# A recurrent block with an MLP and an FP4 gate: the MLP's down projection with the weight stationary, its sum turned by VectorE and through HBM

## The chip, the cores and the metric

The kernel runs on one core of a Trainium2 chip. The metric is the device time of one execution in microseconds (us). TensorE, VectorE, ScalarE, GpSimd and SyncE are called PE, DVE, ACT, POOL and SP, as in the profile; SP issues every DMA of this kernel.

## The reference

Input x has 4 sequences of 1024 tokens with 256 channels. In short:

```
xn = layernorm(x)
x1 = xn + linear_attention(rmsnorm(xn) ...) @ Wo      # 8 heads, chunks of 128 tokens, a carried state
h  = rmsnorm(x1) * mlp_norm_w
s  = x1 + (silu(h @ Wgate) * (h @ Wup)) @ Wdown       # 256 -> 1024 -> 256: the MLP
q  = fp4_linear(xn, w_gate), fp4_linear(xn, w_up)     # 256 -> 704, both operands rounded to FP4 in groups of 16
g  = silu(fp4_linear(silu(q0) * q1, w_down))          # 704 -> 256: the gate
out = x + s * g
```

The change touches the product with `Wdown` and the sum `x1 + ...` behind it.

## The kernel before

The work falls into blocks of 512 tokens (4 chunks of 128), 8 blocks in all. A first stage, up to about 600 us, does layer norm and attention for every block and leaves what the second stage needs in HBM: `kept` (x1 and its factor), `kept_xq` and `kept_h2` (rounded xn and normed x1, each turned in 32 x 32 pieces so that a load puts channels on partitions). The second stage, which the change is about, is one function `networks(n, final)` on each engine, called for n = 0 to 7. There is no scheduler: the order of work on each engine is the order of the program's text, engines meet at semaphores, and SP issues its DMAs strictly in the order in which its own text lists them, waiting in front of each for the semaphores named there.

All products are made of three fp32r matmuls of high and low halves (`split_product`, L250 to L259). In one block n of the second stage PE does, for each chunk c of 128 tokens:

- `gate_up4(n, c)`: the FP4 gate and up products of chunk c, 4 times 6 matmuls of 352 columns;
- `gate_up(n, 2c)` and `gate_up(n, 2c+1)`: slices f = 2c and 2c+1 (128 of the 1024 hidden channels) of the MLP's gate and up products, each over all 512 tokens with the weight stationary: 6 matmuls of 512 columns for gate, 6 for up;
- `down(n, f)` for f = 2c-1 and 2c (L801): the hidden slice f, times `Wdown`, added into PSUM banks `B_MLP` and `B_MLP + 1`. Here the activation `hmT` is stationary, one 128-token chunk at a time, and 256 columns of `wdown` move: 4 chunks times 3, so 12 matmuls of 256 columns for one f. The result lies with tokens on partitions;
- `down4(m)`: the FP4 down projection of the chunk m = 4n + c - 2, two chunks late (`LAG4 = 2`).

`down(n, 7)` ends the block's sum, then `gate_up4(n+1, 0)` begins the next one.

DVE in the same block rounds the hidden values of the FP4 branch (`quantize_scale`, `quantize_apply`, `quantize_constants`, `quantize_add`, `quantize_subtract`, `quantize_done`), multiplies gate and up of both branches (`mlp_product`, L1598 to L1601; `product4`, L1608 to L1612) and makes the low halves (`mlp_lo`, L1605; `hq_lo`, L1618; `xT_lo_of`, L1537). PE's `gate_up(n, f)` waits for `mlp_product(n, f-1)` before its up half, since there is one bank for up, and `down(n, f)` waits for `mlp_lo(n, f)`. At the end of a block DVE adds the MLP's sum to `x2b` (x1, loaded by SP) straight out of PSUM, in one instruction (L1696); POOL then multiplies by the gate and adds x.

The FP4 hidden values make a trip through HBM for each chunk m, `exchange4(m)` on SP (L507 to L520): the store of chunk m (L511), then a wait for that store and for `hq_lo(m-1)` by DVE, since the landing buffer is used again, then four loads (L519):

```
sp.wait_ge(h4_quantized, m + 1)
sp.dma_start(through.rearrange("a p x -> p a x"), h4_turned_sb).then_inc(hq_stored, 16)
sp.wait_ge(hq_stored, 16 * (m + 1))
...
    sp.wait_ge(hqT_ready, m)
```

`hq_lo(m-1)` for the last chunk of a block, m = 4n + 3, stands in DVE's text in the first chunk of the next block. Behind `exchange4(4n + 3)` SP issues the four loads of a later block's `kept_h2` (`load_turned`, L483 to L485).

Of the kernel before, what the change touches and what calls it, by code (L numbers as in the profile page):

```python
# [5 lines left out]
ALU = mybir.AluOpType  # L6
ACT = mybir.ActivationFunctionType
AX_X = mybir.AxisListType.X
F32 = mybir.dt.float32
# [4 lines left out]
P = 128  # L14
BANK = 512
QUAD = 32
QUADS = P // QUAD
# [41 lines left out]
def build(nc, x, attn_w, Wq, Wk, Wv, Wo, out_w, mlp_w, Wgate, Wup, Wdown, w_gate, w_up, w_down, out):  # L59
    batches, tokens, D = x.shape  # L60
    HD = Wq.shape[1]
    H = HD // P
    KD = D // P
    INTER = Wgate.shape[1]
    FT = INTER // P
    N4 = w_gate.shape[0]
    T4 = -(-N4 // P)
# [3 lines left out]
    CH = BANK // P  # L71
    TB = CH * P
    HALVES = tokens // TB
    BLOCKS = batches * HALVES
    STEPS = HALVES * H
# [12 lines left out]
    moved = nc.dram_tensor("moved", (QUADS, P, 2 * CH * QUAD), F32).ap()  # L88
    kept_xq, kept_h2 = (nc.dram_tensor(name, (BLOCKS, QUADS, P, KD * CH * QUAD), F32).ap()
                        for name in ("kept_xq", "kept_h2"))  # L90
    kept_h4 = nc.dram_tensor("kept_h4", (2, QUADS, P, T4 * QUAD), F32).ap()
    PIECE_OF = ((1, 0), (1, 1), (0, 0), (0, 1), (2, 0), (2, 1))
    PIECE4 = (N4, N4, N4, N4, T4 // 2 * D, T4 // 2 * D)
# [3 lines left out]
    with ctx:  # L97
# [3 lines left out]
        def sem(name):  # L101
            return ctx.enter_context(nc.semaphore(name))
# [14 lines left out]
        wdown = r_q[:, :].rearrange("p (a f n) -> p a f n", a=2, f=FT)  # L117


        r_h = sb("r_h", [P, 2 * 2 * KD * TB], F32R)  # L120
# [8 lines left out]
        hmT = hid_r.cut(2, 2, TB)  # L129
# [60 lines left out]
        def turned(tile, k):  # L190

            return tile.rearrange("p (a k c t) -> p k c a t", a=QUADS, k=KD, c=CH)[:, k]

        def landed(tile, k):

            return tile.rearrange("p (b k c t) -> p k c b t", b=QUADS, k=KD, c=CH)[:, k]
# [8 lines left out]
        def in_quads(tile):  # L205
            return tile.rearrange("p (a x) -> p a x", a=QUADS)
# [21 lines left out]
        xb = two.cut(CH, D)  # L228
        res = two.cut(CH, D)
        g4 = two.cut(CH, D)  # L230
        hq_in_last = xq_in[:, 0:QUADS * T4 * QUAD].rearrange("p (a x) -> p a x", a=QUADS)
        hqT_last = r_k[:, 0:2 * T4 * P].rearrange("p (a f n) -> p a f n", a=2, f=T4)
        two.at = x2_end
# [17 lines left out]
        def split_product(pe, out_ap, weight, activation, kinds, first, last, skip=False):  # L251

            for n, (wp, ap) in enumerate(PRODUCTS):
                a, b = activation(ap), weight(wp)
                if kinds == "weight stationary":
                    a, b = b, a
                done = pe.matmul(out_ap, a, b, start=first and n == 0, stop=last and n == 2,  # L259
                                 skip_group_check=skip)  # L260
            return done
# [77 lines left out]
        hq_stored, hq_loaded = sem("hq_stored"), sem("hq_loaded")  # L339
        out4_done, g4_ready = sem("out4_done"), sem("g4_ready")  # L340
        mlp_done, sum_read = sem("mlp_done"), sem("sum_read")
        product_ready, res_ready, out_stored = sem("product_ready"), sem("res_ready"), sem("out_stored")
        dve2 = sem("dve2_done")
        TURNS = 2 * KD
# [31 lines left out]
        with nc.Block() as block:  # L376
            @block.sync
            def _(sp):
# [125 lines left out]
                sp.wait_ge(xT_ready, TURNS)  # L504
                load_turned(h2_in, kept_h2[1], h2_loaded)

                def exchange4(m):  # L507

                    through = kept_h4[m % 2]
                    sp.wait_ge(h4_quantized, m + 1)  # L510
                    sp.dma_start(through.rearrange("a p x -> p a x"), h4_turned_sb).then_inc(hq_stored, 16)  # L511
                    sp.wait_ge(hq_stored, 16 * (m + 1))
                    if m == LAST4 - 1:
                        sp.wait_ge(xT_ready, (BLOCKS - 1) * TURNS + KD)
                    elif m:
                        sp.wait_ge(hqT_ready, m)
                    landing = hq_homes(m)[0]
                    for q in range(QUADS):
                        sp.dma_start(landing[q * QUAD:(q + 1) * QUAD],  # L519
                                     through[q].rearrange("(b p) x -> p b x", b=QUADS)).then_inc(hq_loaded, 16)  # L520

                for n in range(BLOCKS):
                    exchange4(n * CH)
                    if n == 0:
                        sp.wait_ge(wdown_ready, 2)
                        sp.dma_start(xb, x_blocks[0]).then_inc(xb_loaded, 16)
                    if n == 2:
                        sp.wait_ge(h2_turned, BLOCKS + 1)
                        sp.dma_start(kept_h2[BLOCKS - 1].rearrange("a p x -> p a x"),
                                     leaving.rearrange("p a i x -> p a (i x)")).then_inc(h2_stored, 16)  # L530
                    exchange4(n * CH + 1)
                    if n == 0:
                        sp.dma_start(x2b, kept[0][:, :, 0:D]).then_inc(xb_loaded, 16)
                    else:
                        sp.wait_ge(res_ready, n)
                        sp.dma_start(out_blocks[n - 1], res).then_inc(out_stored, 16)
                        sp.dma_start(xb, x_blocks[n]).then_inc(xb_loaded, 16)
                        if n == BLOCKS - 1:
                            sp.wait_ge(x2_stored, 16 * (BLOCKS + 1))
                        sp.dma_start(x2b, kept[n][:, :, 0:D]).then_inc(xb_loaded, 16)  # L540
                    exchange4(n * CH + 2)
                    if n + 2 < BLOCKS:
                        sp.wait_ge(xT_ready, (n + 1) * TURNS + KD)
                        load_turned(xq_in, kept_xq[n + 2], xq_loaded)
                    if n == 1:
                        sp.wait_ge(x2_ready, BLOCKS + 1)
                        sp.dma_start(kept[BLOCKS - 1], x2).then_inc(x2_stored, 16)
                    if n < BLOCKS - 1:
                        exchange4(n * CH + 3)
                    if n + 2 < BLOCKS:  # L550
                        sp.wait_ge(xT_ready, (n + 1) * TURNS + TURNS)
                        sp.wait_ge(h2_stored, 16 * (n + 4))
                        load_turned(h2_in, kept_h2[n + 2], h2_loaded)
# [40 lines left out]
            def _(pe):  # L594
# [205 lines left out]

                def down(n, f):  # L801
                    if f == 0:
                        pe.wait_ge(sum_read, n + 1)
                        pe.wait_ge(wdown_ready, 1)
                        pe.wait_ge(h4_ready, 1)
                    if n == 0 and f == FT // 2:
                        pe.wait_ge(wdown_ready, 2)
                    pe.wait_ge(hmT_ready, n * FT + f + 1)
                    for c in range(CH):
                        done = split_product(pe, ps[:, B_MLP + c // 2, (c % 2) * D:(c % 2 + 1) * D],  # L810
                                             lambda a: wdown[:, a, f, :],
                                             lambda a: hmT[:, f % 2, a, c * P:(c + 1) * P],
                                             "activation stationary", f == 0 and c % 2 == 0, f == FT - 1, skip=True)
                    if f == FT - 1:
                        done.then_inc(mlp_done, 1)
# [384 lines left out]
            def _(dve):  # L1200
# [128 lines left out]
                def turn_blocks(to, data, done_sem):  # L1329

                    for k in range(KD):
                        done = dve.transpose(turned(to, k), by_quads(data, k))
                    done.then_inc(done_sem, 1)
# [293 lines left out]
                                          hqT[:, HI, f0:f1, :].bitcast(F32), ALU.subtract).then_inc(hqT_ready, 1)  # L1627

                dve.sem_inc(sum_read, 1)
                dve.sem_inc(out_stored, 16)  # L1630
                product4(0, 0, 0)
                xT_lo_of(0, range(KD, TURNS))
# [4 lines left out]
                def wdown_lo(i):  # L1637
                    dve.wait_ge(wdown_hi, i + 1)
                    part = slice(i * FT // 2, (i + 1) * FT // 2)
                    dve.tensor_tensor(wdown[:, LO, part, :], raw_wdown[:, part, :], wdown[:, HI, part, :].bitcast(F32),  # L1640
                                      ALU.subtract).then_inc(wdown_ready, 1)

                DVE_BLOCK = CH * (SCALE_STEPS + ROUND_STEPS)

                def networks(n, final):
                    mine = Tally(n * DVE_BLOCK)
                    for c in range(CH):
# [32 lines left out]
                            x2_factor(BLOCKS + 1, before)  # L1680
                        if (n, c) == (2, 0):
                            dve.wait_ge(h2_ready, BLOCKS + 1)
                            dve.wait_ge(o_turned, STEPS - PLAIN - 1)
                            turn_blocks(leaving.rearrange("p a i x -> p (a i x)"), xq_new, h2_turned)
                        if c == 0:
                            product4(n, 1, 0)
                        quantize_subtract(data, mine)
# [3 lines left out]
                    if not final:  # L1691
                        xT_lo_of(n + 1, range(KD, TURNS))
                    dve.wait_ge(mlp_done, n + 1)
                    dve.wait_ge(xb_loaded, 32 * n + 32)
                    dve.wait_ge(out_stored, 16 * n + 16)
                    dve.tensor_tensor(res, ps[:, B_MLP:B_MLP + 2, :].rearrange("p a (c d) -> p (a c) d", d=D),  # L1696
                                      x2b, ALU.add).then_inc(sum_read, 1)
                    if not final:
                        product4(n + 1, 0, 0)
                        product4(n + 1, 0, 1)  # L1700
# [40 lines left out]
```

## Time and profile before

| | us |
|---|---|
| median of 3 runs (1065.27 to 1066.4) | 1065.48 |
| the profiled execution's own time | 1066.6 |
| its span, from the first to the last instruction | 1064.5 |
| PE busy in the span | 1053.9 (99%) |
| DVE busy | 908.8 (85%) |
| ACT busy | 528.1 (50%) |
| POOL busy | 47.4 (4%) |

A busy time is the time in which at least one instruction of the engine runs; a matmul's duration in the profile is that of a pipeline, so the spacing of matmuls is read from when groups of them begin in the timeline, and not from their mean duration. The share of the granted clock is 0.999 over the span. All times in the rows are of one profiled execution, in us from the span's start.

### The profile page before, as it was taken

Reading aid. Unit: us, or ns where it says so; the run is one execution under the profiler, and the core shown is the slowest. Engines: PE = TensorE matmul, PEld = TensorE weight load, DVE = VectorE, ACT = ScalarE, POOL = GpSimd, SP = SyncE. Lnnn points to the kernel's source line nnn. Section 1 sums busy time; section 2 is a strip of 40 time slices with the busy share of each in tenths; the row PEclk is TensorE's granted clock in tenths of the full one; section 3 lists DMA queues with packets and bytes.
Section 4 is the critical chain, followed back from the end, with each engine's and each line's share of the span. In section 5 each row is a group of like instructions: output and inputs, shape, how many; then the busy total and the mean of one; then the engine's idle time right before and its main releaser. Section 6 shows DMA issues by size and latency. Waiting matters only on the chain.

```text
span 1064.5 us, 18767 instructions
## 1 busy us (share of the span) xinstructions
PE 1053.9 (99%) x6794; PEld 961.5 (90%) x6794; DVE 908.8 (85%) x1887; ACT 528.1 (50%) x1490; POOL 47.4 (4%) x68
## 2 busy tenths in 40 slices
PE   9999999999999999999999999999999999999998
PEld 5999999989999989989999889999999999999997
DVE  6788888888888888888888798888888888889887
ACT  6664655756656546557555634443333333243332
POOL 0000000000000000000000000101001010101010
PEclk9999999999999999999999999999999999999999
DMA  7445355455464553653544623253433233423213
GB/s 237 149 159 174 108 173 168 138 157 166 134 192 133 165 171 115 187 170 123 171 148 162 194 66 99 80 158 93 121 90 119 85 120 97 122 84 92 87 57 112
DMA packets 166173, 143.08 MB, mean 134 GB/s; under 512 B 28737, under 2 KB 162881, under 8 KB 166081
## 3 DMA queue, kind: packets, MB, share of 16 engines
q1 hardware_dynamic: 166080, 141.88, 42.7%
q8 instruction: 54, 0.88, 0.4%
q14 instruction: 39, 0.31, 0.1%
HBM read 77.27 MB, written 64.57 MB: 133 GB/s over the span
## 4 chain that ended last, share of the span: by engine, by line
PE 88%; DMA 6%; DVE 2%; ACT 2%; SPq 2%; issue 1%; DVEq 0%
PE ps L259 69%; PE ps L713 5%; PE ps L757 4%; PE ps L751 4%; PE ps L737 4%; DMA moved<-work 3%; DMA r_gate<-moved 2%; SPq L409 1%; PE ps L839 1%; PE ps L598 1%; SPq L481 1%; DMA work<-kept_w 1%; DMA work<-in_L_attn_hidden_states 0%; ACT work L922 0%; DVE work L1473 0%
## 5 line engine op out<-in xcount | busy, mean ns | idle before, releaser
L259 PE MATMUL ps<-r_k,r_gate_up 128*128 128x512 f32 x768 | 185.2, 391 | 0.5 <-DVE r_k L1537 0.5
L259 PEld LDWEIGHTS ps<-r_k,r_gate_up 128*128 128x128 f32 x768 | 141.5, 188 | 27.9 <-issue 0.7
L259 PE MATMUL ps<-r_o,onT 128*128 128x256 f32 x768 | 107.0, 289 | 0.4 <-DVE onT L1265 0.4
L259 PE MATMUL ps<-r_h,r_k 128*128 128x512 f32 (+1 forms) x393 | 105.2, 403 | 0.0
L259 PEld LDWEIGHTS ps<-r_q,r_v 128*128 128x128 f32 x768 | 99.7, 191 | 5.0 <-DVE r_v L1605 0.3
L259 PE MATMUL ps<-r_q,r_v 128*128 128x256 f32 x768 | 102.3, 283 | 0.0
L259 PE MATMUL ps<-r_h,r_q 128*128 128x512 f32 x384 | 98.2, 391 | 0.0
L946 ACT ACTIVATE work<-ps 128x128 f32<-128x128 f32 x256 | 67.0, 276 | 62.8 <-PE ps L757 62.7
L259 PE MATMUL ps<-r_v,r_h 128*128 128x512 f32 x384 | 97.4, 390 | 0.0
L259 PEld LDWEIGHTS ps<-r_o,onT 128*128 128x128 f32 x768 | 95.8, 190 | 0.8 <-DVE onT L1265 0.7
L922 ACT ACTIVATE work<-ps 128x512 f32<-128x512 f32 x64 | 38.3, 599 | 109.3 <-PE ps L259 109.1
L1121 ACT ACTIVATE r_v<-work 128x512 fp32r<-128x512 f32 x64 | 40.5, 633 | 99.8 <-DVE work L1601 99.7
L259 PEld LDWEIGHTS ps<-r_h,r_q 128*128 128x128 f32 x384 | 72.1, 188 | 16.5
L259 PEld LDWEIGHTS ps<-r_v,r_h 128*128 128x128 f32 x384 | 72.1, 188 | 15.0
L1508 DVE TENSOR_TENSOR work<-ps,work 128x128 f32<-128x128 f32 x192 | 55.7, 290 | 26.6 <-ACT work L960 17.1
L259 PEld LDWEIGHTS ps<-r_h,r_k 128*128 128x128 f32 x393 | 68.2, 189 | 11.1
L1117 ACT ACTIVATE work<-ps 128x512 f32<-128x512 f32 x64 | 38.3, 598 | 79.1 <-PE ps L259 79.1
L259 PE MATMUL ps<-r_gate,r_k 128*128 128x352 f32 x384 | 71.8, 322 | 0.0
L259 PE MATMUL ps<-r_up,r_k 128*128 128x352 f32 x384 | 71.6, 322 | 0.0
L751 PE MATMUL ps<-work 128*128 128x128 f32 x512 | 67.7, 275 | 0.4 <-DVE work L1486 0.4
L757 PE MATMUL ps<-work 128*128 128x128 f32 x448 | 65.8, 284 | 1.7 <-DVE work L1508 1.0
L713 PE MATMUL ps<-work 128*128 128x128 f32 x512 | 67.3, 274 | 0.0
(155 smaller groups left out, 1996.1 us busy)
## 6 DMA issues: line engine op xcount, KB each, us to landing
moved<-work SPq DMA_DIRECT2D x63, 512.0 KB, 2.9
r_gate<-moved SPq DMA_DIRECT2D x252, 128.0 KB, 2.5
kept_h<-work SPq DMA_DIRECT2D x31, 384.0 KB, 2.6
work<-kept_h SPq DMA_DIRECT2D x124, 96.0 KB, 2.3
work<-in_L_attn_hidden_states SPq DMA_DIRECT2D x16, 512.0 KB, 5.4
kept<-work SPq DMA_DIRECT2D x9, 514.0 KB, 4.4
kept_h<-work SPq DMA_DIRECT2D x9, 512.0 KB, 3.6
kept_xq<-work SPq DMA_DIRECT2D x8, 512.0 KB, 5.8
```

What stands on the lines that cost most here:

```text
L259: done = pe.matmul(out_ap, a, b, start=first and n == 0, stop=last and n == 2, skip_group_check=skip)
L409: sp.dma_start(arriving[q * QUAD:(q + 1) * QUAD].rearrange("p a i x -> p a (i x)"), moved[q].rearrange("(a p) x -> p a x", a=QUADS)).then_ ...
L481: sp.dma_start(rows[:, f], w[:, :, at:at + QUAD]).then_inc(piece_loaded, 16)
L713: done = pe.matmul(ps[:, B_SCORE, c * P:(c + 1) * P], kT[:, c * P:(c + 1) * P], qT[:, j % 2, c * P:(c + 1) * P], start=True, stop=True)
L737: done = pe.matmul(ps[:, B_STATE, c * P:(c + 1) * P], k_tok[:, c, :], v_sb[:, half, c, hv:hv + P], start=True, stop=True)
L751: pe.matmul(ps[:, B_O, c * P:(c + 1) * P], attn[:, c, :], v_sb[:, half, c, hv:hv + P], start=c == 0, stop=s == 0 and c == 0, skip_group_ch ...
L757: done = pe.matmul(ps[:, B_O, c * P:(c + 1) * P], qT[:, j % 2, c * P:(c + 1) * P], before, start=False, stop=True, skip_group_check=True)
L922: act.activation(kT, ps[:, B_K, :], ACT.Copy).then_inc(k_ready, 1)
L946: done = act.activation(squares[:, c, :], ps[:, B_O, c * P:(c + 1) * P], ACT.Square, accum_out=small[:, OS, c:c + 1])
L1117: act.activation(s_gate, ps[:, B_GATE, :], ACT.Silu).then_inc(s_gate_ready, 1)
L1121: act.activation(hmT[:, f % 2, HI, :], hm, ACT.Copy).then_inc(hm_hi, 1)
L1508: dve.tensor_tensor(to, share, last, ALU.add).then_inc(state_ready, 1)
```

## The change

For blocks 0 to 6 the down projection takes the weight as the stationary operand: for each hidden slice f, two halves of 128 output channels, three matmuls of 512 token columns each, so 6 matmuls of 512 columns where there were 12 of 256. The result then lies with output channels on partitions. At the end of the block DVE turns the two banks in 32 x 32 pieces into the buffer `leaving`, called `m_turned` here (L1740 of the changed kernel), in place of the sum with `x2b`. SP stores that to `kept_m` inside `exchange4(4n + 3, n)` and, behind that exchange's own four loads, issues four loads that land it as `m_in`. DVE adds `m_in` and `x2b` in the first chunk of the next block (`residual2`, called after `mlp_lo(n, 1)` and in front of `product4(n, 1, 0)`). PE's next use of the two banks waits for the turns (`mlp_turned`) and not for the sum. Block 7 is as it was.

```diff
+    kept_m = nc.dram_tensor("kept_m", (2, QUADS, P, KD * CH * QUAD), F32).ap()
...
+        m_turned = leaving.rearrange("p a i x -> p (a i x)")
+        m_in = r_h[:, 2 * T4 * D:2 * T4 * D + CH * D].bitcast(F32)
...
-                def exchange4(m):
+                def exchange4(m, sum_of=None):
 
                     through = kept_h4[m % 2]
                     sp.wait_ge(h4_quantized, m + 1)
                     sp.dma_start(through.rearrange("a p x -> p a x"), h4_turned_sb).then_inc(hq_stored, 16)
+                    if sum_of is not None:
+                        sp.wait_ge(mlp_turned, sum_of + 2)
+                        sp.dma_start(kept_m[sum_of % 2].rearrange("a p x -> p a x"), in_quads(m_turned))\
+                          .then_inc(m_stored, 16)
                     sp.wait_ge(hq_stored, 16 * (m + 1))
...
                     for q in range(QUADS):
                         sp.dma_start(landing[q * QUAD:(q + 1) * QUAD],
                                      through[q].rearrange("(b p) x -> p b x", b=QUADS)).then_inc(hq_loaded, 16)
+                    if sum_of is not None:
+                        sp.wait_ge(sum_read, sum_of + 1)
+                        sp.wait_ge(m_stored, 16 * (sum_of + 1))
+                        load_turned(m_in, kept_m[sum_of % 2], m_loaded)
...
-                        exchange4(n * CH + 3)
+                        exchange4(n * CH + 3, n)
...
                 def down(n, f):
                     if f == 0:
-                        pe.wait_ge(sum_read, n + 1)
+                        pe.wait_ge(mlp_turned, n + 1)
...
+                    if n < BLOCKS - 1:
+                        for i in range(KD):
+                            done = split_product(pe, ps[:, B_MLP + i, :],
+                                                 lambda a: wdown[:, a, f, i * P:(i + 1) * P],
+                                                 lambda a: hmT[:, f % 2, a, :], "weight stationary", f == 0, f == FT - 1)
+                        if f == FT - 1:
+                            done.then_inc(mlp_done, 1)
+                        return
...
+                def residual2(n):
+                    dve.wait_ge(m_loaded, 16 * QUADS * (n + 1))
+                    dve.wait_ge(xb_loaded, 32 * n + 32)
+                    dve.wait_ge(out_stored, 16 * n + 16)
+                    for i in range(KD):
+                        part = slice(i * P, (i + 1) * P)
+                        done = dve.tensor_tensor(res[:, :, part].rearrange("p c (a e) -> p c a e", e=QUAD), landed(m_in, i),
+                                                 x2b[:, :, part].rearrange("p c (a e) -> p c a e", e=QUAD), ALU.add)
+                    done.then_inc(sum_read, 1)
...
+                        if c == 0 and n:
+                            residual2(n - 1)
                         if c == 0:
                             product4(n, 1, 0)
...
+                        for i in range(KD):
+                            done = dve.transpose(turned(m_turned, i),
+                                                 ps[:, B_MLP + i, :].rearrange("p (c a t) -> p c a t", c=CH, a=QUADS))
+                        done.then_inc(mlp_turned, 1)
```

On SP, around the end of block 2 and the start of block 3 (`kept_h` is the profile's name for `kept_h4` and `kept_h2`; of 192 elements `kept_h4`, of 256 `kept_h2`), before:

```order
L485 DMA work<-kept_xq 32x4x256 x4
L511 DMA kept_h<-work 128x4x192
L519 DMA work<-kept_h 32x4x192 x4
L485 DMA work<-kept_h 32x4x256 x4
L511 DMA kept_h<-work 128x4x192
```

and now:

```order
L489 DMA work<-kept_xq 32x4x256 x4
L515 DMA kept_h<-work 128x4x192
L518 DMA kept_m<-work 128x4x256
L527 DMA work<-kept_h 32x4x192 x4
L489 DMA r_h<-kept_m 32x4x256 x4
L489 DMA work<-kept_h 32x4x256 x4
L515 DMA kept_h<-work 128x4x192
```

The store of the turned sum stands between the exchange's store and its loads, and its four loads stand where the four loads of `kept_h2` stood.

On DVE, in the first chunk of block 3 from `hq_lo` to the product of the MLP's slice 2, before:

```order
L1618 TENSOR_TENSOR r_v<-work,r_v 128x768
L1568 TENSOR_SCALAR work<-work 128x704
L1570 TENSOR_SCALAR work<-work 128x704
L1601 TENSOR_TENSOR work<-ps,work 128x512
L1573 TENSOR_TENSOR work<-work 128x704
L1605 TENSOR_TENSOR r_v<-work,r_v 128x512
L1612 TENSOR_TENSOR work<-ps,work 128x352
L1578 TENSOR_TENSOR work<-work 128x704
```

and now:

```order
L1638 TENSOR_TENSOR r_v<-work,r_v 128x768
L1588 TENSOR_SCALAR work<-work 128x704
L1590 TENSOR_SCALAR work<-work 128x704
L1621 TENSOR_TENSOR work<-ps,work 128x512
L1593 TENSOR_TENSOR work<-work 128x704
L1625 TENSOR_TENSOR r_v<-work,r_v 128x512
L1670 TENSOR_TENSOR work<-r_h,work 128x4x128 x2
L1632 TENSOR_TENSOR work<-ps,work 128x352
L1598 TENSOR_TENSOR work<-work 128x704
```

The two additions of `residual2` (L1670) stand between `mlp_lo(n, 1)` and `product4(n, 1, 0)`; the rest keeps its order.

## Rows read from the trace of the kernel before

**Rows 1.** The page: busy time of each engine, and the granted clock in 40 slices.
```profile
PE 1053.9 (99%) x6794; PEld 961.5 (90%) x6794; DVE 908.8 (85%) x1887; ACT 528.1 (50%) x1490; POOL 47.4 (4%) x68
...
PEclk9999999999999999999999999999999999999999
```
**Rows 2.** Busy time by windows, 57 us long: wall, PE, PEld, DVE, ACT, POOL, clock, DMA.
```profile
828.00:885.00 57.00, 57.00 (x359) 53.04 (x359) 49.52 (x82) 20.08 (x36) 6.34 (x8) 1.00 0.34 103
```
**Rows 3.** Timeline of PE, first chunks of block 3: start, us, line, operation, count.
```profile
774.77 5.63 PE L259 MATMUL ps<-r_k,r_gate_up 128*128 128x512 f32 x24
780.24 1.59 PE L259 MATMUL ps<-r_q,r_v 128*128 128x256 f32 x12
...
787.53 2.91 PE L259 MATMUL ps<-r_k,r_gate_up 128*128 128x512 f32 x12
790.28 1.59 PE L259 MATMUL ps<-r_q,r_v 128*128 128x256 f32 x12
791.71 2.91 PE L259 MATMUL ps<-r_k,r_gate_up 128*128 128x512 f32 x12
794.46 1.59 PE L259 MATMUL ps<-r_q,r_v 128*128 128x256 f32 x12
```
**Rows 4.** Timeline of DVE, end of block 2 and first chunks of block 3.
```profile
772.25 1.25 DVE L1537 TENSOR_TENSOR r_k<-work,r_k 128x512 fp32r<-128x512 f32 x2
773.42 1.22 DVE L1696 TENSOR_TENSOR work<-ps,work 128x1024 f32<-128x1024 f32 x1
...
777.77 0.69 DVE L1601 TENSOR_TENSOR work<-ps,work 128x512 f32<-128x512 f32 x1 [0.45 <-PE ps L259]
...
779.91 0.95 DVE L1618 TENSOR_TENSOR r_v<-work,r_v 128x768 fp32r<-128x768 f32 x1
...
783.30 0.69 DVE L1605 TENSOR_TENSOR r_v<-work,r_v 128x512 fp32r<-128x512 f32 x1
785.83 0.53 DVE L1612 TENSOR_TENSOR work<-ps,work 128x352 f32<-128x352 f32 x1 [1.85 <-PE ps L259]
...
791.68 0.69 DVE L1601 TENSOR_TENSOR work<-ps,work 128x512 f32<-128x512 f32 x1 [0.29 <-DVE work L1561]
...
793.21 0.69 DVE L1605 TENSOR_TENSOR r_v<-work,r_v 128x512 fp32r<-128x512 f32 x1
```
**Rows 5.** One source line: DVE's turns of 128 x 512 out of SBUF, ns.
```profile
L1332 DVE STREAM_TRANSPOSE work<-work x34: 666/670/715, 69.2 to 727.7; 128x512 f32<-128x512 f32 x34
```
**Rows 6.** Waits of SP's queue in the second stage: us in total, times, longest.
```profile
SPq L516 <- DVE r_v L1618: 200.5, 29, 8.1
```
**Rows 7.** Timeline of SP's issues at the starts of blocks 1, 3, 5 and 6.
```profile
667.21 1.73 SPq L519 DMA_DIRECT2D work<-kept_h  x4
669.03 2.56 SPq L485 DMA_DIRECT2D work<-kept_h  x4
...
772.35 0.38 SPq L511 DMA_DIRECT2D kept_h<-work  x1
780.94 1.73 SPq L519 DMA_DIRECT2D work<-kept_h  x4
782.76 1.80 SPq L485 DMA_DIRECT2D work<-kept_h  x4
...
894.65 3.02 SPq L519 DMA_DIRECT2D work<-kept_h  x4
897.77 1.80 SPq L485 DMA_DIRECT2D work<-kept_h  x4
...
951.51 2.61 SPq L519 DMA_DIRECT2D work<-kept_h  x4
954.22 1.81 SPq L485 DMA_DIRECT2D work<-kept_h  x4
```
**Rows 8.** One source line, L485's loads of 128 KB each: us from issue to landing.
```profile
DMA to landing us min/median/max: 2.2/2.7/6.0
```
**Rows 9.** The page's DMA issues: count, KB each, median us to landing.
```profile
kept_h<-work SPq DMA_DIRECT2D x9, 512.0 KB, 3.6
```

More of the change, by code:

```diff
@@ L341, in build @@
         mlp_done, sum_read = sem("mlp_done"), sem("sum_read")
+        mlp_turned, m_stored, m_loaded = sem("mlp_turned"), sem("m_stored"), sem("m_loaded")
         product_ready, res_ready, out_stored = sem("product_ready"), sem("res_ready"), sem("out_stored")
@@ L1629, in _ @@
                 dve.sem_inc(sum_read, 1)
+                dve.sem_inc(mlp_turned, 1)
                 dve.sem_inc(out_stored, 16)
@@ L1682, in networks @@
                             dve.wait_ge(h2_ready, BLOCKS + 1)
-                            dve.wait_ge(o_turned, STEPS - PLAIN - 1)
+                            dve.wait_ge(m_stored, 16 * 2)
                             turn_blocks(leaving.rearrange("p a i x -> p (a i x)"), xq_new, h2_turned)
+                        if c == 0 and n:
+                            residual2(n - 1)
                         if c == 0:
@@ L1693, in networks @@
                     dve.wait_ge(mlp_done, n + 1)
[L1694 to L1697, printed above, removed]
+                    if final:
+                        dve.wait_ge(xb_loaded, 32 * n + 32)
+                        dve.wait_ge(out_stored, 16 * n + 16)
+                        dve.tensor_tensor(res, ps[:, B_MLP:B_MLP + 2, :].rearrange("p a (c d) -> p (a c) d", d=D),
+                                          x2b, ALU.add).then_inc(sum_read, 1)
+                    else:
+                        if n:
+                            dve.wait_ge(m_stored, 16 * n)
+                        else:
+                            dve.wait_ge(o_turned, STEPS - PLAIN - 1)
+                        if n == 2:
+                            dve.wait_ge(h2_stored, 16 * (BLOCKS + 1))
+                        for i in range(KD):
+                            done = dve.transpose(turned(m_turned, i),
+                                                 ps[:, B_MLP + i, :].rearrange("p (c a t) -> p c a t", c=CH, a=QUADS))
+                        done.then_inc(mlp_turned, 1)
                     if not final:
```

## The prediction

> **What bounds the kernel now.** The page comes first. PE is busy for 1053.9 of 1064.5 us and its granted clock stays at the top of its two levels, 2.4 GHz, in every slice [rows 1]. The windows then show one block's length of the second stage: PE is busy in all of 57.00 us, DVE in 49.52 [rows 2]. So there is no wait on PE to be won back. PE's own work there sets the time, and what delays PE by a microsecond costs a microsecond. DVE has 7.5 us to spare in 57, but it sits in particular places, and those decide. The timelines of PE and DVE over the start of block 3 show where [rows 3, 4]. DVE waits 0.45 us for PE before the product of slice 0 (L1601 at 777.77), 1.85 us before `product4(3, 1, 0)` (L1612 at 785.83) and 0.29 us later on. The waits of SP's queue give the last piece. Its loads of the FP4 chunk stand behind `hq_lo` (L1618 of DVE) 29 times, for 200.5 us [rows 6]: SP, which issues in order, is held there until DVE has passed that instruction.
>
> **What PE gains.** In the timeline one `down` of 12 matmuls of 256 columns takes 791.71 - 790.28 = 1.43 us, and 12 matmuls of 512 columns take 794.46 - 791.71 = 2.75 us, so 6 of them 1.375 [rows 3]. One `down` gets 0.055 us shorter. There are 8 in each of 7 blocks: 56 x 0.055 = **3.1 us** less work on PE. The nearest row for the new form is that of the MLP's gate and up products, which have the same shape, the weight stationary too, and a new weight for each matmul; I take it whole.
> The Trainium skill (TensorE: Matmul & The Clock Gate, "Back-to-back issue gap") gives an isolated warm matmul N / 2.4 + 2.5 ns, 109 and 216 ns for 256 and 512 columns, where the rows give 119 and 229; by its figures a `down` would gain 15 ns, the 56 of them an estimated 0.8 us, and the sum below would come out 2.3 us higher. Its section says that a stream with weight loads is paced otherwise, so I stay with the rows.
>
> **What DVE does at a block's end.** Out: one sum out of PSUM, 1.22 us [rows 4]. In: two turns of 128 x 512. The trace turns that size out of SBUF in 0.67 us [rows 5], never out of PSUM. An addition of 512 elements takes 0.69 us with an operand in PSUM (L1601) and without one (L1605) [rows 4], so I take 0.67 each, 1.34 together, 0.12 more than before. The lower end is the same; as upper end I allow twice that, 1.34 us more. The 0.12 lies in DVE's wait of 0.45 us at 777.77, which PE, about 0.17 us earlier by three shorter `down`s, leaves at about 0.16. It costs nothing; the upper end would use up the wait and delay what follows by 0.9 to 1.2 us.
>
> **What SP does.** The store of 512 KB (like the 3.6 us of [rows 9]) is issued when the turns are done, about 774.8 in the times of block 3, and lands near 778.5, when SP is still held: `hq_lo` ends at 779.91 + 0.95 = 780.86 [rows 4] and SP's first load is issued at 780.94 [rows 7]. So the store is hidden. Its loads are not. They are issued behind the four loads of that exchange, in the place that the loads of `kept_h2` have now, with the same sizes, and the trace shows what a second set of four in this place does [rows 7]. From the first issue of the first set to the end of the second set's issues it took 4.38, 3.63, 3.62, 3.80, 4.92 and 4.52 us at the starts of blocks 1 to 6 (the rows show the first, the third, the fifth and the last of the six); the mean is 4.15. The last issue begins some 0.45 us before that end (1.80 / 4), and such a load lands 2.7 us after its issue, at least 2.2 [rows 8]. The turned sum is therefore in SBUF at 780.94 + 4.15 - 0.45 + 2.7 = **787.3**, in block 3's times. `kept_h2`, now behind it, is wanted only at the block's end, some 35 us on; it costs nothing.
>
> **Where DVE then stands.** It reaches `residual2` when `mlp_lo(3, 1)` ends, at 783.30 + 0.69 = 783.99 [rows 4]. It waits there for 3.3 us. Then come two additions, the same shapes as the pair of L1537, whose successor starts 1.17 us after it; with the handover I count 1.25 (lower end 1.2, upper end 1.5, if two operands of 4 dimensions are slower). `product4(3, 1, 0)` starts at 788.6 in place of 785.83: its wait of 1.85 us for PE is gone, but 2.8 us come in. Had the data been there in time, the 1.25 us would have disappeared in the 1.85. Everything behind in DVE's order moves: from `product4(3, 1, 0)` to the end of the product of slice 2 it takes 791.68 + 0.69 - 785.83 = 6.54 us, less the 0.29 of waiting 6.25. That product ends at **794.84**; now it ends at 792.37.
>
> **What waits for it.** PE's up half of slice 3 needs it, as there is one up bank. The group that begins at 791.71 has the gate half first (1.375 us), so the up half begins at 793.08 [rows 3], and 0.11 earlier with two `down`s shortened since slice 0: 792.97. PE waits 794.84 - 792.97 = 1.87 us, and 0.08 for the handover (as SP's, 780.86 to 780.94). Next, `mlp_lo(3, 2)` ends 793.90 - 792.37 = 1.53 us after the product, while the up half takes 1.375: `down(3, 2)` waits a further 0.15. The other waits of that chunk have room: `hq_lo` and the third slice's low half finish well before PE wants them, and the old DVE waits of the later chunks take up what DVE is still behind. So PE stands still for **2.1 us**, once in each of blocks 1 to 7, since `residual2` is called in those seven: 14.7 us. POOL, which multiplies after `residual2`, needs the gate of the last chunk anyway (out of a later `down4`); it costs nothing.
>
> **The sum.** -3.1 + 14.7 = +11.6 us on the profiled execution's own 1066.6, 1078.2; the median of the runs is 1.1 lower, so **1077.1 us**. Bounds: with the shortest issue (3.62) and the earliest landing (2.2) each stall is 1.0 us shorter, 7 less in all, 1070.1; with the longest issue (4.92) for every block 0.8 longer, 1082.5; the slow turns would add up to 8 to that.
>
> **The rivals.** *It hides, and the gain stays.* If the turned sum is in SBUF by about 784.6, so that the additions end inside the 1.85 us, nothing is late on PE and 3.1 us are gained: **1062.4**. For it: the store is done two microseconds before, and four loads are small. Against it: they would have to land 3.7 us after `hq_lo`, while in the trace a second set's last issue alone begins 3.2 us behind the first issue at best [rows 7]. This decides the sign: the point is a landing about 4.8 us after `hq_lo` (a stall of about 0.45 us pays back the gain), against 6.4 forecast. Chance 0.08; of a time within 0.2% (2.1 us, about what a measurement of this kernel can tell) 0.05.
> *DVE cannot catch up.* All of the 2.8 us by which `product4` moves, and the 0.15, come through to PE: 7 x 2.95 - 3.1 = +17.5, **1083.0**. For it: DVE's 49.5 busy us grow to 50.9, and 3.3 us of waiting make it 54.2 of PE's 56.6. Against it: some 2.4 us of room are left, and PE's old schedule at slice 3 had 0.7 us to spare. Chance 0.07.
> *The wide matmuls gain nothing.* If the new form ran at the narrow one's rate per column, 6 x 0.239 = 1.43, the 3.1 us would not come: **1080.2**. For it is only that no row has this weight in this place; against it is the row of the same shape. Chance 0.04. The rule of the skill named above, 0.8 us of gain, belongs here and by an estimate gives 1079.4.
>
> **How the numbers follow.** The forecast, a stall of 1 to 3 us in seven blocks, has 0.76; with the two slower rivals 0.87. The range leaves out the hidden case and the even one, 0.13, and little more: its low end is the sum with the earliest landings, its high end the slower rival, 1070 to 1083. Faster by over 0.2%: 0.08; within 0.2%: 0.05; slower: 0.87.
>
> **What would show it.** In the profile after: 336 matmuls of 512 columns with `r_q` as the weight and 96 of 256 columns left, spaced 229 and 119 ns; DVE idle for about 3.3 us before the two additions in each of blocks 1 to 7, ended by the DMA from `kept_m`; the loads of `kept_m` issued directly behind those of the exchange, which still wait for `hq_lo`; PE idle for about 2 us at the up half of slice 3, ended by DVE's product (L1621), seven times, and 0.15 before the next `down`; a block length of some 58.5 us. I am wrong if the loads from `kept_m` land before DVE reaches the additions, or if PE's group at slice 3 begins without a gap although DVE is late.

## The result and the profile after

The changed kernel takes 1090.97 us (median of 4 runs, 1089.43 to 1092.72) against 1065.94 for the kernel before in the same comparison: a ratio of 1.0233, 95% interval 1.0216 to 1.0250. It is slower by 25.0 us, about twice the 11.6 that were forecast, and outside the range. The profiled execution took 1089.43 us of its own, with a span of 1087.7.

The page of the changed kernel: engines, then three groups of instructions (busy time, mean ns, idle time in front and what ended most of it).

```profile
PE 1059.9 (97%) x6458; PEld 950.1 (87%) x6458; DVE 923.9 (85%) x1908; ACT 526.8 (48%) x1490; POOL 53.9 (5%) x68
...
L262 PE MATMUL ps<-r_k,r_gate_up 128*128 128x512 f32 x768 | 189.6, 396 | 19.7 <-DVE work L1621 19.2
...
L262 PE MATMUL ps<-r_v,r_q 128*128 128x512 f32 x336 | 90.0, 405 | 0.0
...
L598 POOL TENSOR_TENSOR work<-work 128x256 f32<-128x256 f32 x28 | 30.0, 1092 | 973.5 <-DVE work L1670 902.0
```

PE, which hardly waited in the second stage (busy in all of a block's 57.00 us [rows 2]), now has 19.2 us of idle time in front of its gate and up products, ended by DVE's product (L1621). The 336 wide matmuls are there. POOL's products take 1092 ns on average. The waits of the second stage, on DVE and on PE (total us, times, longest), name the other end of the chain:

```profile
DVE work L1670 <- DMA r_h<-kept_m: 22.9, 7, 4.6
```
```profile
PE ps L262 <- DVE work L1621: 19.2, 7, 3.9
```

Seven times DVE stands for 3.27 us on average at the two additions until the loads of the turned sum land, and seven times PE stands for 2.74 us. SP's issues at the start of block 3, the place of [rows 7]:

```profile
779.13 0.38 SPq L518 DMA_DIRECT2D kept_m<-work  x1
785.20 1.75 SPq L527 DMA_DIRECT2D work<-kept_h  x4
787.04 1.80 SPq L489 DMA_DIRECT2D r_h<-kept_m  x4
```

The store leaves at 779.13, and SP then stands for almost six microseconds, until DVE's `hq_lo` lets the exchange's loads go. The loads of the turned sum follow those, at 787.04. DVE at the same place, which answers to [rows 4]:

```profile
777.80 1.30 DVE L1740 STREAM_TRANSPOSE work<-ps 128x512 f32<-128x512 f32 x2
...
784.17 0.95 DVE L1638 TENSOR_TENSOR r_v<-work,r_v 128x768 fp32r<-128x768 f32 x1
...
791.18 1.29 DVE L1670 TENSOR_TENSOR work<-r_h,work 128x512 f32<-128x512 f32 x2 [2.93 <-DMA r_h<-kept_m]
792.39 0.52 DVE L1632 TENSOR_TENSOR work<-ps,work 128x352 f32<-128x352 f32 x1
792.83 1.22 DVE L1598 TENSOR_TENSOR work<-work 128x704 f32<-128x704 f32 x1
794.08 1.32 DVE L1603 TENSOR_TENSOR work<-work 128x704 f32<-128x704 f32 x1
...
798.73 0.69 DVE L1621 TENSOR_TENSOR work<-ps,work 128x512 f32<-128x512 f32 x1
```

The turns out of PSUM and the additions cost what was expected. The two rounding steps behind them (L1598 and L1603) do not: 1.22 and 1.32 us, where their medians over the kernel are 0.88 and 0.89. POOL's timeline shows what runs at that moment: its products now start when the additions are done.

```profile
792.55 3.44 POOL L598 TENSOR_TENSOR work<-work 128x256 f32<-128x256 f32 x3 [42.74 <-DVE work L1670]
```

PE's timeline, which answers to [rows 3]: the group of 24 that opens each of blocks 1 to 7, the group behind each of the seven waits, and for block 3 what lies between.

```profile
657.75 5.64 PE L262 MATMUL ps<-r_k,r_gate_up 128*128 128x512 f32 x24
...
678.22 1.65 PE L262 MATMUL ps<-r_k,r_gate_up 128*128 128x512 f32 x6 [2.15 <-DVE work L1621]
679.75 1.66 PE L262 MATMUL ps<-r_v,r_q 128*128 128x512 f32 x6
681.24 1.96 PE L262 MATMUL ps<-r_h,r_v 128*128 128x256 f32 x15
...
716.66 5.76 PE L262 MATMUL ps<-r_k,r_gate_up 128*128 128x512 f32 x24
...
739.25 2.93 PE L262 MATMUL ps<-r_k,r_gate_up 128*128 128x512 f32 x6 [3.93 <-DVE work L1621]
741.98 1.77 PE L262 MATMUL ps<-r_v,r_q 128*128 128x512 f32 x6
...
779.02 5.64 PE L262 MATMUL ps<-r_k,r_gate_up 128*128 128x512 f32 x24
...
794.46 1.52 PE L262 MATMUL ps<-r_v,r_q 128*128 128x512 f32 x6
795.82 1.52 PE L262 MATMUL ps<-r_k,r_gate_up 128*128 128x512 f32 x6
799.48 2.10 PE L262 MATMUL ps<-r_k,r_gate_up 128*128 128x512 f32 x6 [2.13 <-DVE work L1621]
...
839.34 5.64 PE L262 MATMUL ps<-r_k,r_gate_up 128*128 128x512 f32 x24
...
860.56 1.81 PE L262 MATMUL ps<-r_k,r_gate_up 128*128 128x512 f32 x6 [2.87 <-DVE work L1621]
...
900.46 5.64 PE L262 MATMUL ps<-r_k,r_gate_up 128*128 128x512 f32 x24
...
920.85 1.66 PE L262 MATMUL ps<-r_k,r_gate_up 128*128 128x512 f32 x6 [2.06 <-DVE work L1621]
...
959.28 5.65 PE L262 MATMUL ps<-r_k,r_gate_up 128*128 128x512 f32 x24
...
980.06 1.84 PE L262 MATMUL ps<-r_k,r_gate_up 128*128 128x512 f32 x6 [2.44 <-DVE work L1621]
...
1019.95 5.65 PE L262 MATMUL ps<-r_k,r_gate_up 128*128 128x512 f32 x24
...
1042.04 2.29 PE L262 MATMUL ps<-r_k,r_gate_up 128*128 128x512 f32 x6 [3.58 <-DVE work L1621]
```

In the kernel before, the group that opens block 4:

```profile
831.63 5.63 PE L259 MATMUL ps<-r_k,r_gate_up 128*128 128x512 f32 x24
```

The wide `down` takes 795.82 - 794.46 = 1.36 us, against 1.43 for the narrow one. Blocks 1 to 6 take 58.91, 62.36, 60.32, 61.12, 58.82 and 60.67 us, the distances between the groups of 24; block 3 of the kernel before took 831.63 - 774.77 = 56.86 [rows 3]. Take the wait away: blocks 1 and 5 are left with 56.76 each, but blocks 2, 3, 4 and 6 with 58.43, 58.19, 58.25 and 58.23. These four hold about 1.5 us more that is no wait. The rows behind the waits show it: in block 1 six matmuls of 512 columns take 1.53 us from 678.22 to 679.75, in block 2 they take 2.73 from 739.25 to 741.98. The windows give the reason (wall, PE, PEld, DVE, ACT, POOL, granted clock, DMA): in block 3 the wait, then the stretch behind it, and the same in block 5.

```profile
797.00:800.40 3.40, 1.26 (x6) 0.79 (x5) 3.23 (x7) 0.94 (x2) 0.00 (x0) 1.00 0.34 116
800.50:803.80 3.30, 3.30 (x9) 2.56 (x8) 3.23 (x6) 0.30 (x2) 0.00 (x0) 0.50 0.21 59
...
918.00:921.00 3.00, 0.94 (x5) 0.47 (x4) 2.83 (x7) 0.17 (x1) 0.00 (x0) 1.00 0.38 131
921.00:924.40 3.40, 3.40 (x17) 2.65 (x18) 3.30 (x6) 0.94 (x2) 0.00 (x0) 1.00 0.03 8
```

Behind the wait of block 3 the granted clock is 0.50, the lower of its two levels, 1.2 GHz, while PE is fully busy again; behind that of block 5 it stays at 2.4 GHz. Block 7 shows the low clock as well, so five of the seven waits were followed by it. The page hides this: its slices are 27 us long, and its row of the clock is 9 throughout for the changed kernel too.

A wait also costs more than the idle time that the profile counts. Blocks 1 and 5 kept the full clock, and the 56.76 us that they are left with are 0.46 more than a block with the wide matmuls and no wait (56.30, in the runs below). Part of it can be seen: the group behind the wait of block 3 begins 799.48 - 795.82 = 3.66 us after the one in front, 1.36 of work and 2.30, where 2.13 are counted as idle; and the two groups of six behind the wait of block 1 take 1.53 and 681.24 - 679.75 = 1.49 instead of 1.36.

The sum then: waits 19.2; what seven waits cost beyond their idle time at 0.46, 3.2; five stretches of the low clock at about 1.5, 7.5; less the gain of the wide matmuls, 3.6 by their own run below. That is +26.3, against 484.4 - 458.3 = 26.1 measured between the two traces from the first slice of the MLP to the end.

### The profile page after: what moved, and what is told of

It is laid out like the page before. It is cut to its first block, busy times and chain, and to the rows that moved or that the text cites. A ratio compares the mean times of both kernels' runs of the same rounds, so it can differ in the third digit from the quotient of the medians.

```text
span 1087.7 us, 18166 instructions
## 1 busy us (share of the span) xinstructions
PE 1059.9 (97%) x6458; PEld 950.1 (87%) x6458; DVE 923.9 (85%) x1908; ACT 526.8 (48%) x1490; POOL 53.9 (5%) x68
## 4 chain that ended last, share of the span: by engine, by line
PE 76%; DVE 9%; DMA 6%; SPq 4%; issue 2%; ACT 2%; DVEq 0%
PE ps L262 58%; PE ps L725 5%; PE ps L769 4%; PE ps L763 4%; PE ps L749 4%; DMA moved<-work 2%; DMA r_h<-kept_m 2%; DMA r_gate<-moved 1%; SPq L527 1%; DVE work L1621 1%; SPq L489 1%; DVE work L1603 1%; SPq L413 1%; DVE work L1598 1%; DVE work L1632 1%
## 5 line engine op out<-in xcount | busy, mean ns | idle before, releaser
L262 PE MATMUL ps<-r_k,r_gate_up 128*128 128x512 f32 x768 | 189.6, 396 | 19.7 <-DVE work L1621 19.2
L262 PEld LDWEIGHTS ps<-r_k,r_gate_up 128*128 128x128 f32 x768 | 143.5, 189 | 51.4 <-DVE work L1621 22.9
L262 PE MATMUL ps<-r_v,r_q 128*128 128x512 f32 x336 | 90.0, 405 | 0.0
L598 POOL TENSOR_TENSOR work<-work 128x256 f32<-128x256 f32 x28 | 30.0, 1092 | 973.5 <-DVE work L1670 902.0
L262 PEld LDWEIGHTS ps<-r_v,r_q 128*128 128x128 f32 x336 | 64.6, 196 | 15.5 <-DVE r_v L1625 1.5
L763 PE MATMUL ps<-work 128*128 128x128 f32 x512 | 67.7, 275 | 0.5 <-DVE work L1506 0.5
L725 PE MATMUL ps<-work 128*128 128x128 f32 x512 | 67.3, 274 | 0.0
```

The source lines that it names most:

```text
L598: pool.tensor_tensor(res[:, c, :], res[:, c, :], g4[:, c, :], ALU.mult).then_inc(product_ready, 1)
L725: done = pe.matmul(ps[:, B_SCORE, c * P:(c + 1) * P], kT[:, c * P:(c + 1) * P], qT[:, j % 2, c * P:(c + 1) * P], start=True, stop=True)
L763: pe.matmul(ps[:, B_O, c * P:(c + 1) * P], attn[:, c, :], v_sb[:, half, c, hv:hv + P], start=c == 0, stop=s == 0 and c == 0, skip_group_ch ...
```

## The experiments

Theory: one chain. The turned sum lands late, since its loads stand in SP's order behind a wait for `hq_lo`; DVE stands at the additions; POOL's products start when they end and slow DVE's next steps; PE waits for DVE at slice 3; and in most blocks its clock falls after that. The main rival was that DVE, with two turns and two additions more in a block, has simply become the bound. Each ratio is to the kernel before, run beside the edits: its median was 1065.32 us beside POOL later, the loads first, no trip and PE kept busy, and 1065.99 beside the others, so the times of the two groups can be compared only to about 1 us, besides the interval of each.

**POOL one chunk later** (1082.05 us, ratio 1.0155, 1.0122 to 1.0187).

```diff
                     for c in range(CH):
-                        pool.wait_ge(g4_ready, n * CH + c + 2)
+                        pool.wait_ge(g4_ready, n * CH + CH + 1)
```

> Edit: POOL starts the four products of a block only when the gate of the block's last chunk is there, one chunk after the sum, so that none of them runs beside DVE's first chunk. Theory (a stall chain: late landing of the turned sum, then DVE slowed by POOL's products running beside it, then PE waits 2.74 us on average, then the granted clock falls): DVE's two quantize steps behind the sum (subtract and scale of 704 elements) go back from 1.22 and 1.32 us to 0.88 and 0.89, PE's wait at the up half of slice 3 falls from 19.2 us in all to about 13.7, the time to about 1085, lower (to 1078) if clock drops vanish too. Rival (the slow DVE steps come from the DMA traffic of the moment, not from POOL): they stay at 1.2 and 1.3, and the time stays at 1091.

The two rounding steps are back at their usual times, with the wait at the additions unchanged (22.4 us in all). DVE's timeline at block 3, and PE's waits:

```profile
788.69 1.29 DVE L1670 TENSOR_TENSOR work<-r_h,work 128x512 f32<-128x512 f32 x2 [3.17 <-DMA r_h<-kept_m]
...
790.34 0.88 DVE L1598 TENSOR_TENSOR work<-work 128x704 f32<-128x704 f32 x1
791.25 0.89 DVE L1603 TENSOR_TENSOR work<-work 128x704 f32<-128x704 f32 x1
```
```profile
PE ps L262 <- DVE work L1621: 13.3, 7, 3.1
```

So POOL, not the DMA traffic, made them slow: SP issues the same loads in the same order and at the same distances here. PE's waits fall by 5.9 us, 0.84 a block, and with the shorter waits three of the five clock falls go, in the profiled execution, which with 1078.18 us is the shortest of the four. The wait that is left, 1.90 us a block, is close to the 1.95 of the prediction (1.87 and 0.08 for the handover).

**The turned sum's loads first** (1063.80 us, ratio 0.9981, 0.9968 to 0.9994).

```diff
                         sp.dma_start(kept_m[sum_of % 2].rearrange("a p x -> p a x"), in_quads(m_turned))\
                           .then_inc(m_stored, 16)
+                        sp.wait_ge(sum_read, sum_of + 1)
+                        sp.wait_ge(m_stored, 16 * (sum_of + 1))
+                        load_turned(m_in, kept_m[sum_of % 2], m_loaded)
                     sp.wait_ge(hq_stored, 16 * (m + 1))
...
-                    if sum_of is not None:
-                        sp.wait_ge(sum_read, sum_of + 1)
-                        sp.wait_ge(m_stored, 16 * (sum_of + 1))
-                        load_turned(m_in, kept_m[sum_of % 2], m_loaded)
```

> Edit: on SP alone, the four loads of the turned sum are issued directly behind its store, ahead of the wait for DVE's low half of the FP4 hidden values and of that exchange's loads. Theory: the loads go out about 3.6 us after the store, 2 to 3 us earlier than now, and land before DVE comes to the two additions; the additions hide in DVE's old wait for PE, PE has no wait at slice 3, the clock does not fall, and the gain of the wide matmuls is left: 1062, faster than before by 3 to 4 us. Rival (VectorE's extra work, two turns and two additions, makes it the bound, wherever the loads stand): PE still waits over 1 us a block and the time stays above 1072.

The store, the loads, the turns and the additions are all still there; only the order on SP differs, and the change turns from 25 us slower into slightly faster than the kernel before. SP at the start of block 3, then DVE's additions, now without a wait:

```profile
773.97 0.38 SPq L518 DMA_DIRECT2D kept_m<-work  x1
776.94 1.75 SPq L489 DMA_DIRECT2D r_h<-kept_m  x4
780.02 1.73 SPq L530 DMA_DIRECT2D work<-kept_h  x4
```
```profile
782.99 1.29 DVE L1669 TENSOR_TENSOR work<-r_h,work 128x512 f32<-128x512 f32 x2
784.86 0.53 DVE L1631 TENSOR_TENSOR work<-ps,work 128x352 f32<-128x352 f32 x1 [0.59 <-PE ps L262]
785.30 1.23 DVE L1597 TENSOR_TENSOR work<-work 128x704 f32<-128x704 f32 x1
```

The loads leave 3 us behind the store, in the time in which SP stood before. The rival is out: DVE even waits 0.59 us for PE behind the additions. The time misses the 1062 expected by 1.8 us: POOL still slows the rounding step (1.23), and PE has two waits of 0.3 us; the run with both edits below shows that this is POOL's.

**Without the trip** (1063.14 us, ratio 0.9982, 0.9968 to 0.9996): the store, the loads and the waits for them taken out, DVE's work left in.

> Edit: the store and the loads of the turned sum and every wait for them are left out; DVE's turns and additions stay, the additions read what lies in the landing buffer (the sum of the MLP is left out of seven blocks). Theory: no stall at slice 3, clock at the top throughout, 1062 (1065.9 less 56 products of 0.07 us each). Rival (VectorE is the bound by its own work): above 1070. A second rival (POOL beside DVE alone stalls PE, without any landing): PE waits up to 0.8 us a block, 1066 to 1068.

It is as fast as the kernel with the loads first. The trip through HBM has no price of its own where it is not waited for; PE waits 0.6 us for DVE's product in all of the second stage, so POOL beside DVE alone costs little while DVE has its old room (2 to 3 us, against the run with both edits below).

**PE kept busy in its wait** (1083.81 us, ratio 1.0179, 1.0142 to 1.0215).

```diff
                     swiglu(wgate, B_GATE, f, gate_done)
+                    if n and f == 3:
+                        for i in range(18):
+                            pe.matmul(ps[:, B_OUT4, D:2 * D], wdown[:, HI, 0, 0:P], wdown[:, HI, 0, :], start=True,
+                                      stop=True)
                     if n or f:
```

> Edit: 18 matmuls of 256 columns into unused columns of a PSUM bank are put on PE in front of its wait for DVE at the up half of slice 3 of blocks 1 to 7, about 2.15 us of work inside the wait. Theory (the granted clock falls because PE stands idle there): PE's idle time in that place falls from 19.2 us to about 4, nothing ends earlier or later in the chain, but the five stretches of the lower clock disappear or become one or two; each costs some 1.6 us of a block, so the time falls by 5 to 8 us, to 1083 to 1086. Rival (the falls are not tied to the idle time): five falls remain, 1091 or more.

The chain of waits is the same, DVE stands 23.2 us at the additions, but PE's waits are filled (4.4 us are left), and the low clock is gone. Windows over 600 to 1080 us, first of this kernel, then of the changed one:

```profile
600.00:1080.00 480.00, 473.40 (x2660) 423.35 (x2659) 420.88 (x691) 168.81 (x309) 56.07 (x56) 1.00 0.37 112
```
```profile
600.00:1080.00 480.00, 460.29 (x2500) 408.99 (x2499) 414.42 (x679) 166.12 (x302) 50.80 (x56) 0.98 0.37 111
```

Work that computes nothing makes the kernel 7.2 us faster than the change by the medians, 1.4 us for each of the five falls. By the two ratios it is 5.8, give or take some 4, as one of the four runs took 1089.13, at the full clock like the others; why is open. The two traces, from the first slice of the MLP (604.32) to the end, give 484.4 - 477.9 = 6.5. The falls came from PE standing idle. The Trainium skill (TensorE: Matmul & The Clock Gate, "Why this matters for your kernels") asks that TensorE not be left idle between bursts of matmuls, because its clock goes back to the lower level. The traces agree: five falls behind seven waits, none once the waits are filled. But the idle time that its row allows is longer than the 2.13 us after which the clock fell in block 3; the measurement decides.

**The turned sum's loads ahead of the exchange's, behind the same wait** (1069.38 us, ratio 1.0028, 1.0016 to 1.0040): on SP, the four loads moved to between the wait for `hqT_ready` and the exchange's four loads.

> Edit: on SP, the loads of the turned sum stay behind the wait for DVE's low half, but ahead of that exchange's own four loads. They are issued about 1.9 us earlier than in the change. Theory (PE's wait follows the landing one for one): DVE's wait falls from 3.3 to about 1.4 us a block, PE's from 2.74 to about 0.9, at most two clock falls: 1067 to 1073. Rival (contention, not the place in the queue, makes the landing late): the wait stays over 2.5 us and the time over 1080.

The first of these loads is issued where the exchange's first load stood, 1.84 us earlier than in the change (787.04 - 785.20), and DVE's wait at the additions goes from 22.9 to 7.9 us in all, 2.1 less a block:

```profile
DVE work L1670 <- DMA r_h<-kept_m: 7.9, 7, 1.8
```

PE's waits go from 19.2 to 4.1, and the granted clock does not fall. So the time follows the place in the queue; DMA contention did not make the landing late. This kernel is close to the point where the sign turns: 0.6 us of wait a block, with the 0.46 that each costs beyond it, comes to more than the wide matmuls give.

**The wide matmuls alone** (1062.95 us, ratio 0.9967, 0.9957 to 0.9977): the kernel before with the new `down` for blocks 0 to 6, DVE adding the banks as before.

> Edit: the kernel before, with the wide matmuls of blocks 0 to 6 alone; DVE adds the two banks as before, without turning them (so the MLP's sum of seven blocks is added at the wrong places). It measures what PE gains by itself. By the rows of before 0.055 us for each of 56 products, 3.1 us: 1062.2; by the spacing in the trace of the change (1.36 us for 6 matmuls) 0.07 each, 3.9 us: 1061.4. Rival (the wide form gains nothing): 1065.3.

PE's group of 24 in blocks 1 and 2:

```profile
663.64 5.65 PE L259 MATMUL ps<-r_k,r_gate_up 128*128 128x512 f32 x24
...
719.97 5.64 PE L259 MATMUL ps<-r_k,r_gate_up 128*128 128x512 f32 x24
```

Block 1 takes 56.33 us instead of 56.86, and blocks 2 to 6 take 56.30 each: a gain of 0.53 to 0.56 a block. From the first slice of the MLP (609.06) to the end it is 458.3 - 454.7 = 3.6 us, as block 0 gains less. By the medians it is 3.0, and the interval of the ratio is 2.5 to 4.6 us.

**Both edits, loads first and POOL later** (1061.11 us, ratio 0.9951, 0.9937 to 0.9966).

> Edit: both edits of the earlier runs, the loads of the turned sum directly behind its store and POOL's products one chunk later. Theory: the kernel with the loads first still had DVE's two quantize steps at 1.2 and 1.3 us, which left waits of 0.3 us on PE and blocks of 56.56 to 57.4 us; with POOL moved the steps go to 0.88 and 0.89, every block takes about 56.4 us, and the time is 1061.5 to 1062.5, some 1 to 2 us under the loads-first kernel. Rival (POOL, later, holds SP's store of the result and the loads behind it): no gain over the loads-first kernel's 1063.8, or a loss.

The gain of the wide matmuls arrives, and PE has no wait for DVE's product any more. Blocks 1 and 4, by the same group:

```profile
657.73 5.65 PE L262 MATMUL ps<-r_k,r_gate_up 128*128 128x512 f32 x24
714.10 5.75 PE L262 MATMUL ps<-r_k,r_gate_up 128*128 128x512 f32 x24
...
827.09 5.64 PE L262 MATMUL ps<-r_k,r_gate_up 128*128 128x512 f32 x24
883.39 5.64 PE L262 MATMUL ps<-r_k,r_gate_up 128*128 128x512 f32 x24
```

Block 1 takes 56.37 and block 4 56.30 us, as with the wide matmuls alone; only block 2 takes more, 56.66. This version beats both kernels.

**The additions one chunk later** (1061.23 us, ratio 0.9958, 0.9944 to 0.9973): SP and POOL as in the change.

```diff
-                        if c == 0 and n:
+                        if c == 1 and n:
                             residual2(n - 1)
```

> Edit: the order on SP stays that of the change; DVE's two additions stand in the second chunk of the next block and not in the first, about 13 us later. Theory (the change loses by one landing some 3 us too late for where it is read): DVE no longer waits for the landing, PE has no wait at slice 3 and the clock stays up: 1062 to 1064. Rival (POOL's products now end so late that SP waits for them in front of the next loads, and the FP4 chunk arrives late): over 1066.

One character is enough. The landing is where it was, but it is read some 13 us later; DVE no longer waits for the landing, PE no longer for DVE's product, the clock stays up, and the rival's late POOL holds nobody back. POOL's products still run beside DVE, in the second chunk, and slow one step there (L1603, 1.31 us in block 3), but nothing waits for it. This version and the one before it are within each other's intervals.

## Why the prediction was right or wrong

- **What bounds the kernel**: right. PE had no wait to give back, and the waits that came onto it came out whole in the time, and 0.46 us each on top.
- **What PE gains**: 3.1 us by the rows of another product of the same shape; the wide matmuls alone gave 3.6 by the traces, 3.0 by the medians. Right within the noise. The estimated 0.8 us by the Trainium skill's isolated spacing was further off.
- **DVE at a block's end**: right, 1.30 us for the two turns out of PSUM (1.34 forecast), and they cost nothing.
- **SP and the landing**: right. Forecast 787.3, 6.4 us behind the end of `hq_lo`; in the trace the additions begin 791.18 - 785.12 = 6.1 us behind it in block 3, and the mean wait of DVE over the seven blocks is 3.27 us (3.3 forecast).
- **POOL "needs the gate of the last chunk anyway; it costs nothing"**: the first step that failed. I looked at when POOL finishes and who waits for it, and not at what it does to its neighbour while it runs. The chain from `product4` to slice 2's product took 7.03 us (792.39 to 799.42), not 6.25, and the two steps beside POOL make up the difference (0.34 and 0.43). The shift of POOL's products alone showed 5.9 us of waits, and clock falls that hang on their length.
- **The sum without a term for the clock**: the second step that failed. I read a granted clock at the top over the whole trace of before and carried it over to a kernel with a new idle time on PE. Five falls cost 7.5 us by the blocks of the trace, 7.2 by the medians of the run that filled the waits. What a wait costs beyond its idle time, 3.2 us in all, had no term either.
- **The stall's own size**: right where it stands alone. With POOL moved PE waited 1.90 us a block at the up half of slice 3, 1.95 forecast. The further 0.15 us before the next `down` did not come: PE has no idle time in front of the wide matmuls (0.0 in the page's row).
- **The rivals**: the hidden landing was priced at 1062.4 and, once SP's order let it happen, measured at 1061.1 to 1063.8. The point from which it decides was put at a wait of 0.45 us on PE; at 0.6 the kernel was slower by 0.28%, and as each wait costs 0.46 more than its idle time, the point lies nearer to no wait at all. "DVE cannot catch up" had a stall of 2.95 us, near the 2.74 that came, but by another mechanism: with POOL moved the landing was as late (22.4 us of waits on DVE) and PE waited 1.90, so DVE did catch up.

By the medians 13.4 us were missing from the sum (25.0 against 11.6), by the two traces 14.5 (26.1). About 6 are POOL beside DVE, about 7 the clock and 3 what the waits cost beyond their idle time; against these stand 1.0 us for the 0.15 that did not come and 0.5 of gain more than forecast. POOL and the clock overlap, since the longer wait also brings the fall more often.

## What to carry to other kernels

A transfer's place in an in-order queue is part of its price: ask what the queue waits for in front of it, and lay the consumer behind the landing that follows from that; here moving four loads past one wait, or the consumer by one chunk, was worth 27 to 30 us. When a stall on TensorE is forecast, add to its length: what else starts at the moment at which the late data arrives and runs beside the critical engine, the lower clock that can follow the idle time, and the slower start of the work behind it.

## What the runs showed of the hardware

- POOL and DVE slow each other when both read SBUF: DVE's two steps of 704 elements with both operands in SBUF (L1598, L1603) went from 0.88 and 0.89 to 1.22 and 1.32 us, while the median of POOL's products of 256 went from 0.74 in the trace of before to 1.26. The Trainium skill (SBUF — State Buffer, "Who interferes with whom") says that a DVE instruction with two SBUF inputs contends with a GpSimd instruction that reads SBUF. The traces agree: with POOL's products moved to the next chunk, the two steps of the first are back at 0.88 and 0.89.
- The granted clock fell after five of the seven waits, of 2.13, 2.44, 2.87, 3.58 and 3.93 us, and not after those of 2.06 and 2.15. With POOL moved it fell after the two longest waits, 3.06 and 2.41 us, and not after the five of at most 1.90; with the loads ahead of the exchange's, where no wait is over 1.02 us, it never fell.
- The first stage, which no edit here touches, is not equally long in all executions: PE's first slice of the MLP begins at 603.25 us in the changed kernel's trace and at 606.20 in that of before. Differences below 3 us between two single executions are read by blocks or by medians.
